# A selective-scan block: dt spread for two units at a time on the two 64-row halves of TensorE, with four dt banks and a dense ring of two

## What is computed

```python
x = x + block(layernorm(x))      # block(u): h = u + mamba(rmsnorm(u)); h + mlp(rmsnorm(h))
x = x + ffn(layernorm(x))        # silu(x W1) * (x W3), Walsh-Hadamard transform, times W2
# mamba: z, x, B, C, dt_raw = split(u @ in_proj); dt = softplus(dt_raw @ dt_proj + b)
# 8 groups of 32 channels p, 32 states n:
#   h[g,p,n] = exp(dt[g,p] * A[g,p,n]) * h[g,p,n] + dt[g,p] * x[g,p] * B[g,n]     (step by step in time)
#   y[g,p]   = sum_n h[g,p,n] * C[g,n]
# y = (y + x * D) * silu(z), then out_proj; mlp: down(silu(gate) * up), 704 wide
```

## Time and profile before

| | us |
|---|---|
| median of 3 executions | 1326.49 |
| the profiled execution, its own time | 1327.35 |
| its span in the trace | 1325.6 |
| PE busy | 1094.1 (83%) |
| DVE busy | 1101.3 (83%) |
| POOL busy | 977.7 (74%) |
| ACT busy | 626.5 (47%) |

### The profile page before, as it was taken

The page is one execution under the profiler, slowest core; times in us unless marked ns, Lnnn a source line. Parts: engine busy times, 40 slices in busy tenths (PEclk is TensorE's granted clock), DMA queues, the critical chain, the costliest instruction groups (busy, mean ns, idle before and its releaser), DMA issues.

```text
span 1325.6 us, 14750 instructions
## 1 busy us (share of the span) xinstructions
PE 1094.1 (83%) x3848; PEld 551.6 (42%) x3848; DVE 1101.3 (83%) x1265; ACT 626.5 (47%) x1070; POOL 977.7 (74%) x596
## 2 busy tenths in 40 slices
PE   2476658999798987999698987999698988998888
PEld 1121123445344453435344453445344454445445
DVE  3389998899889998999889998999989998997222
ACT  3645455445554455545554454545554355442310
POOL 0489997877879786877888786877888788875100
PEclk9776779999899997999899997999899998999889
DMA  5797866655665657575756647574756557550000
GB/s 194 175 236 157 186 153 133 141 131 124 161 143 128 143 134 162 119 158 118 170 133 138 140 119 167 122 167 103 177 129 145 118 132 167 127 127 32 1 0 17
DMA packets 99512, 176.56 MB, mean 133 GB/s; under 512 B 12960, under 2 KB 21600, under 8 KB 98784
## 3 DMA queue, kind: packets, MB, share of 16 engines
q1 hardware_dynamic: 98272, 171.36, 56.2%
q0 software_dynamic: 1152, 4.19, 0.9%
HBM read 150.34 MB, written 8.39 MB: 120 GB/s over the span
## 4 chain that ended last, share of the span: by engine, by line
PE 34%; POOL 27%; issue 21%; ACT 7%; DVE 6%; DMA 3%; SPq 1%; POOLq 0%; DVEq 0%; ACTq 0%
POOL h_s L980 16%; PE p_r L456 9%; PE p_r L467 6%; PE p_r L462 6%; POOL bt_s L960 5%; PE p_dt L411 4%; PE p_y L422 3%; PE p_r L442 2%; DVE h_s L760 2%; DMA bt_s<-dx_rows 2%; PE p_r L473 2%; PE p_r L437 1%; ACT p_dt L549 1%; POOL carry L977 1%; POOL sp_l L994 1%
## 5 line engine op out<-in xcount | busy, mean ns | idle before, releaser
L980 POOL TENSOR_TENSOR h_s<-h_s,c_s 128x1024 f32<-128x1024 f32 x256 | 608.3, 2377 | 127.5 <-DVE h_s L760 117.2
L549 ACT ACTIVATE p_dt<-p_dt,an_s 128x512 f32<-128x512 f32 x512 | 333.1, 657 | 334.0 <-PE p_dt L411 333.5
L411 PE MATMUL p_dt<-kdt,pick_s 128*128 128x512 f32 x512 | 357.6, 704 | 106.9 <-DVE h_s L760 105.0
L760 DVE TENSOR_TENSOR_SCAN h_s<-p_dt,carry,bt_s 128x512 f32<-128x512 f32 x256 | 322.2, 1272 | 25.3 <-ACT p_dt L549 20.3
L760 DVE TENSOR_TENSOR_SCAN h_s<-p_dt,bt_s 128x512 f32<-128x512 f32 x256 | 304.9, 1210 | 31.0 <-ACT p_dt L549 17.7
L467 PE MATMUL p_r<-nT,w_s 128*128 128x512 f32 x512 | 243.2, 602 | 0.4 <-ACT nT L686 0.4
L960 POOL TENSOR_TENSOR bt_s<-bt_s,b_s 128x1024 f32<-128x1024 f32 x96 | 226.7, 2361 | 10.9 <-DMA bt_s<-dx_rows 10.5
L411 PEld LDWEIGHTS p_dt<-kdt,pick_s 128*128 128x128 f32 x512 | 103.4, 204 | 264.8 <-DVE h_s L760 180.7
L745 DVE TENSOR_TENSOR bt_s<-bt_s,p_b 128x1024 f32<-128x1024 f32 x160 | 192.7, 1204 | 4.5 <-issue 2.8
L456 PE MATMUL p_r<-nT,gu_s 128*128 128x512 f32 x352 | 169.4, 602 | 0.3 <-DVE th_s L905 0.3
L422 PE MATMUL p_y<-h_s,ysel_s 128*32 128x512 f32 x1024 | 150.6, 663 | 18.8 <-POOL h_s L980 18.8
(11 more groups left out here) (93 smaller groups left out, 900.7 us busy)
## 6 DMA issues: line engine op xcount, KB each, us to landing
bt_s<-dx_rows SPq DMA_DIRECT2D x512, 256.0 KB, 5.3
kdt<-st_dt SPq DMA_DIRECT2D x64, 128.0 KB, 3.2
tok<-in_x SPq DMA_DIRECT2D x8, 512.0 KB, 7.1
xr_s<-xb_s SPq DMA_DIRECT2D x64, 64.0 KB, 2.4
dx_rows<-sp_w SPq DMA_DIRECT2D x16, 256.0 KB, 2.0
b_s<-xb_s SPq DMA_DIRECT2D x64, 64.0 KB, 2.5
xo<-in_x SPq DMA_DIRECT2D x8, 512.0 KB, 3.9
out<-xo POOLq DMA_DIRECT2D x8, 512.0 KB, 3.4
```

The source lines that it names most:

```text
L411: nc.tensor.matmul(p_dt[DT_BANK[u]][:, :], sel, kdt[:, h, p // 16, :], start=True, stop=True)\
L549: A(p_dt[DT_BANK[u]][:, :], p_dt[DT_BANK[u]][:, :], ACT.Exp, scale=an_s[:, c:c + 1]).then_inc(a_dA, 1)
L760: V.tensor_tensor_scan(h_s[:, u % 8, :], p_dt[DT_BANK[u]][:, :], bt_s[:, u % 16, :], carry[:, u:u + 1] if par else 0.0, ALU.mult, ALU.add) ...
L980: G.tensor_tensor(h_s[:, two, :], h_s[:, two, :], c_s[:, h, :].unsqueeze(1).broadcast_to([P, 2, T]), ALU.mult)\
```

## The change

- Spread by pairs: in each even slot u PE issues units u + 2 and u + 3 together. One uses rows 0 to 63 of TensorE, the other rows 64 to 127 (`pick_s` and `kdt` sliced by 64 partitions), into two different banks of four.
- `kdt` is laid out anew, so that each 64-partition half holds high and low part of 32 rows; `load_dt` issues eight DMAs of 32 partitions in place of four of 64. `pick_s` is half as large and is loaded by four DMAs of together half the bytes in place of one.
- A pair waits until the scans of the units four and three back are over, at every place of a tile.
- PSUM has 8 banks: four for dt, one each for B and y, and two in place of three for the dense ring. The stages keep their slots.

```diff
-DT_BANK = [u % 3 for u in range(U - 1)] + [1]
-DT_GAP = [4, 2] + [3] * (U - 3) + [2]
...
-RING = 3
+RING = 2
...
-        p_dt = [bank(f"p_dt{k}") for k in range(3)]
+        p_dt = [bank(f"p_dt{k}") for k in range(4)]
...
-            sp.dma_start(bt_s[:, 0:4, :].rearrange("p a b -> p (a b)"), pick).then_inc(l_w["c"], 16)
+            for k in range(4):
+                quarter, part = slice(32 * k, 32 * k + 32), k % 2 * 1024
+                sp.dma_start(bt_s[quarter, 0:2, :].rearrange("p a b -> p (a b)"), pick[quarter, part:part + 1024])\
+                  .then_inc(l_w["c"], 16)
...
                 for part in range(2):
                     for q in range(2):
-                        sp.dma_start(kdt[64 * part:64 * part + 64, h, q, :].bitcast(F32),
-                                     st_dt[64 * q:64 * q + 64, part, :].bitcast(F32)).then_inc(l_k[h], 16)
+                        for b in range(2):
+                            dst, src = 64 * b + 32 * part, 64 * q + 32 * b
+                            sp.dma_start(kdt[dst:dst + 32, h, q, :].bitcast(F32),
+                                         st_dt[src:src + 32, part, :].bitcast(F32)).then_inc(l_k[h], 16)
...
-            def spread(i, u):
-
-                h, p = u // UH, unit_channel(u)
-                n = i * U + u
-                sel = pick_s[:, p % 16, :]
+            def spread_pair(i, u):
+
+                h, q, row, n = u // UH, u % 4 // 2, unit_channel(u) % 8, i * U + u
                 if u % UH == 0:
-                    pe.wait_ge(l_k[h], (i + 1) * 64)
-                if u >= 3 or from_tile(i, 1):
-                    pe.wait_ge(v_sc, n - DT_GAP[u] + 1)
-                nc.tensor.matmul(p_dt[DT_BANK[u]][:, :], sel, kdt[:, h, p // 16, :], start=True, stop=True)\
-                    .then_inc(pe_dt, 1)
+                    pe.wait_ge(l_k[h], (i + 1) * 128)
+                if u >= 4 or from_tile(i, 1):
+                    pe.wait_ge(v_sc, n - 2)
+                for b in range(2):
+                    half = slice(64 * b, 64 * b + 64)
+                    nc.tensor.matmul(p_dt[u % 4 + b][:, :], pick_s[half, row, :], kdt[half, h, q, :],
+                                     start=True, stop=True).then_inc(pe_dt, 1)
...
-                    if (units if u + 2 < U else pre):
-                        spread(i + (u + 2) // U, (u + 2) % U)
+                    if u % 2 == 0 and (units if u + 2 < U else pre):
+                        spread_pair(i + (u + 2) // U, (u + 2) % U)
```

More of the change, by code:

```diff
@@ L133, in build @@
         ident_s = sb("ident_s", [P, P])
-        pick_s = sb("pick_s", [P, 16, P], F32R)
+        pick_s = sb("pick_s", [P, 8, P], F32R)
         ysel_s = sb("ysel_s", [P, 60])
@@ L483, in transform_w2 @@
                 for k in range(4):
-                    ps = ring[k] if k < RING else p_y
+                    ps = ring[k] if k < RING else p_dt[k]
                     nc.tensor.matmul(ps[:, :], had_s, hd_s[:, 4 + k, :], start=True, stop=True).then_inc(w_w2, 1)
@@ L510, in _ @@
             pe.wait_ge(w_in, 2)
-            pe.wait_ge(l_w["c"], 80)
+            pe.wait_ge(l_w["c"], 128)
             bodies(pe, body)
@@ L522, in _ @@
                 A(in_s[:, k, :, :], in_s[:, k, :, :], ACT.Copy, scale=par_s[:, k:k + 1]).then_inc(w_in, 1)
-            act.wait_ge(l_w["c"], 80)
+            act.wait_ge(l_w["c"], 128)
             A(an_s[:, :], an_s[:, :], ACT.Exp).then_inc(w_an, 1)
@@ L541, in keep_w2 @@
                     act.wait_ge(w_w2, k + 1)
-                    src = (ring[k] if k < RING else p_y)[:, :].rearrange("p (b d) -> p b d", d=D)
+                    src = (ring[k] if k < RING else p_dt[k])[:, :].rearrange("p (b d) -> p b d", d=D)
                     A(w2_s[:, 2 * k:2 * k + 2, :], src, ACT.Copy).then_inc(w_w2c, 1)
@@ L548, in decay @@
                 c = UH * (u // UH) + unit_channel(u)
-                A(p_dt[DT_BANK[u]][:, :], p_dt[DT_BANK[u]][:, :], ACT.Exp, scale=an_s[:, c:c + 1]).then_inc(a_dA, 1)
+                A(p_dt[u % 4][:, :], p_dt[u % 4][:, :], ACT.Exp, scale=an_s[:, c:c + 1]).then_inc(a_dA, 1)
             def normalise(dst, src, scale, bias, signal):
@@ L586, in softplus @@
                     if h:
-                        act.wait_ge(l_k[0], (t + 1) * 64)
+                        act.wait_ge(l_k[0], (t + 1) * 128)
                     elif from_tile(t, 1):
-                        act.wait_ge(l_k[1], t * 64)
+                        act.wait_ge(l_k[1], t * 128)
                     act.wait_ge(g_dt, m + 1)
@@ L720, in _ @@
             dve.wait_ge(w_zero, 2)
-            dve.wait_ge(l_w["c"], 80)
+            dve.wait_ge(l_w["c"], 128)
             V.tensor_copy(pick_s[:, :, :].rearrange("p a b -> p (a b)"),
-                          bt_s[:, 0:4, :].rearrange("p a b -> p (a b)")).then_inc(w_pick, 1)
+                          bt_s[:, 0:2, :].rearrange("p a b -> p (a b)")).then_inc(w_pick, 1)
             def butterflies():
@@ L759, in scan @@
                     dve.wait_ge(pe_y, i * (U // 4) + u // 4 - 1)
-                V.tensor_tensor_scan(h_s[:, u % 8, :], p_dt[DT_BANK[u]][:, :], bt_s[:, u % 16, :],
+                V.tensor_tensor_scan(h_s[:, u % 8, :], p_dt[u % 4][:, :], bt_s[:, u % 16, :],
                                      carry[:, u:u + 1] if par else 0.0, ALU.mult, ALU.add).then_inc(v_sc, 1)
@@ L845, in body @@
                                 if h:
-                                    dve.wait_ge(l_k[0], (nt + 1) * 64)
+                                    dve.wait_ge(l_k[0], (nt + 1) * 128)
                                 elif from_tile(nt, 1):
-                                    dve.wait_ge(l_k[1], nt * 64)
+                                    dve.wait_ge(l_k[1], nt * 128)
                                 dve.wait_ge(a_dth, m + 1)
```

## The result

| | before | changed |
|---|---|---|
| median of 4 runs each, us | 1326.45 (1325.91 to 1327.89) | 1379.56 (1371.93 to 1384.34) |
| profiled execution, us | 1327.35 | 1371.93 |
| its span, us | 1325.6 | 1370.2 |
| mean granted PE clock | 0.919 | 0.895 |

The changed kernel is slower: ratio 1.0393, 95% interval 1.0345 to 1.0441, or +53 us. The forecast was 1346 us with a range up to 1366. The two profiles of it are +44.6 and +54.8 us over that of before; both are used.

What follows compares the result with a forecast made beforehand. It took PE and DVE to run neck and neck in the dense stages. Seven bodies (19.3 us), tail 1.3 and start 1.4, less 2 gained, made +20.0 on the median of 1326.49: 1346 us, range 1329 to 1366.

Steps and rivals of the forecast that it cites:

- w2: First w2 matmul waits for the read of w3 7, costing 0.25 us a tile.
- The ring of two: Stages wait for the reader two back; at gate 4 PE stands 2.4 us, charged at 1.7 us a tile.
- Tail: In the last body gate 4 and w2 0 each stand for one DVE read: 1.3 us.
- w1/w3: the new wait costs nothing: In w1/w3 the smallest slack before a needed read is 0.30 us, so the shorter ring costs nothing.
- z and the transposes: I charge nothing: z 0 and hT 1 wait for readers, but PE idles there for the norm chain: no charge.
- The pair of spreads: In w1/w3, a half-array pair between full matmuls takes 0.67 us, 0.21 more than before: 0.8 us a tile.
- the start: At the run's start, extra load_dt DMA issues cost 2.4 us, the pick load saves 1: +1.4 us.
- What is gained: At the tile's end the last w2 matmuls no longer stand behind PE's wait for scan 61: -2 us.
- Rival 1: The halves don't overlap: in w1/w3 and gate stages each pair costs 0.23 us more, 1364 us; chance 0.13.
- 3 (faster): Early spreads remove half of the scans' 38.0 us waiting and gate 4's bank is free in time: 1312 us; chance 0.12.
- Rival 2: The ring wait at gate 4 is hidden because DVE is late there: 7 x 1.7 us less, 1334 us; chance 0.17.

Runs made afterwards that it cites:

- e1: Kernel before with only the dense ring cut from three banks to two, one bank left unused: 1368.48 us, ratio 1.0316.
- e12: Kernel before with a ring of two, the idle bank serving as third ring bank for gate, up and dtp0 only: 1343.94 us, ratio 1.0138.
- e8: Kernel before with dtp0 moved ahead of gate 0 in the plan: 1345.01 us, ratio 1.0136.
- e6: Kernel before, without pairs, each spread alone on a 64-row half with the new layouts and loads: 1421.15 us, ratio 1.0711.
- e10: Kernel before with two xo buffers by tile parity, so loading x needn't wait for the last tile's store: 1327.21 us, ratio 1.0013.
- e2: Changed kernel with every spread on all 128 rows and the old layouts and loads: 1365.37 us, ratio 1.0305; repeated, 1363.40 us.
- e11: Changed kernel with two xo buffers by tile parity, so loading x needn't wait for the last tile's store: 1376.91 us, ratio 1.0378.
- e9: Changed kernel with each pair's matmuls issued three times in the bodies of tiles -1, 0 and 1: 1385.09 us, ratio 1.0428.
- e4: Kernel before with DVE's drive reading B from SBUF instead of the PSUM copy, ACT's copies dropped: 1488.02 us, ratio 1.1186.

## Why the prediction was wrong

The direction and most mechanisms were right; the sum came out at +20 where +53 was measured, and +49.7 in the mean of the changed kernel's two profiles. The 29.7 us between lie by the table in gate 3 (7.4 against nothing), in the tile's change with slots 63 and 0 to 12 together (+6.9 against -2), before w2 (5.7 against 1.75), in w1/w3 (8.3 against 5.6), in the tail (4.0 against 1.3), in gate 4 (14.0 against 11.9) and in smaller parts. No term of the sum has the clock. Point by point, with the table's numbers for e1 (the ring alone) and for the changed kernel:

- **"The ring of two", gate 4: right in size.** Forecast 1.7 us a tile from a 2.4 us hold; the change shows 1.35 and 1.77 in slots 22 to 25 of tiles 1 to 6, after a wait of 1.78. 7 x 1.7 = 11.9 stands against 10.6 (e1) and 13.2. The way was not quite the one forecast: scan 25 waits for ACT 0.64 us longer and not 1.7, the rest lies in the waits before scan 23 (0.68) and before DVE's read of gate 4 (0.74), and dtp0 has no wait for a read.
- **"The ring of two", gate 3: left out. This is the step that failed first.** I compared w1 4, gate 4, w2 and z with their readers, and not gate 3. The trace of before had it, in the same stretch as the earlier trace rows:

```profile
530.55 1.88 PE L456 MATMUL p_r<-nT,gu_s 128*128 128x512 f32 x4
531.97 0.66 DVE L905 SCALAR_TENSOR_TENSOR th_s<-th_s,p_r 128x512 f32<-128x512 f32 x1
```

  The last two of the four passes are gate 3; they began at 530.55 + 0.86 = 531.4, and the read of gate 2, whose bank they take with a ring of two, ended at 532.63, 1.2 us later. I had seen only that "gate 3 is read until 537.35". It costs 0.8 to 0.9 us a tile in e1 and about 1.0 in the change, since a state sum stands behind it and the scan waits for that: 6.0 and 7.4 us in slots 19 to 22 against nothing in the sum.
- **"Tail" and the seventh body: too small.** The sum had 7 like bodies and 1.3 us of tail. Tile 7 has 3.5 us in slots 22 to 25 and 2.0 before w2, where tiles 1 to 6 have about 1.5 and 0.45. The gate 4 wait of tile 7 is 2.75 us, and the clock takes 1.1 of the 3.5 (e1, where it did not fall there, has 2.4). The tail is 3.7 (4.3 in e1, 1.7 in e12). Runs with a ring of three have +0.8 (e8), -1.4 (e6) and -2.8 (e10) in the tail, so its parts are no firmer than some 2 us.
- **"w1/w3: the new wait costs nothing": nearly.** No wait of PE for a read is recorded there, and e1 and e12 have 0.4 us in slots 40 to 44 of each of the tiles 2 to 6, 2.0 in all. There DVE waits 0.66 us for ACT's tanh before its read of a w1 stage (593.21 in e1's timeline) where it waited 0.27 before: DVE arrives earlier against PE, and no bank is waited for.
- **"w2": 0.25 us forecast, 0.3 to 0.5 measured**, 5.7 in all against 1.75.
- **"z and the transposes: I charge nothing", the cover being the norm chain: right for the ring alone but for tile 1, wrong for the change.** Slots 0 to 12 cost 4.7 in e1, of which 3.3 are tile 1, and 3.5 in e12, all of it in tile 1; 2.3 of that lie in slots 3 to 6, where the first profile of the changed kernel has 0.1. With pairs they cost 8.7 and 12.7 (e2), in the change 10 and 15. In the row at 667.20 PE stands 2.59 us for the out block's add before z 0, as named, with DVE's and ACT's own chain behind. The load of x sets a small part of it at most: e11 gains 3.2 us there in three tiles.
- **"The pair of spreads": sizes right, sum too small.** 0.63 against 0.67 for a pair, 9.12 against 9.20 for four slots, the overlap real (two 64-row spreads are 0.50 us of busy PE together, and e1's timeline has 0.50 for one full spread where nothing runs beside it). In slots 36 to 48 of tiles without a fall of the clock the ring costs 0.39 us, the pairs on full rows 0.25 more (e2) and the halves 0.40 more (changed): 0.65 for pairs on halves against 0.8 forecast. But the halves cost 15 us by medians, against a forecast of 5.6 for the pairs and 1.4 for the start. The table shows 8.9 of them between the means of the two profiles each (49.7 and 40.9): 3.3 in slots 36 to 48, 2.4 in 12 to 19 (1.3 of it in tile 0, at the clock of 0.5; e9, where the clock came back, has none of that; for the rest I charged nothing "since PE will stand there anyway"), 1.2 before w2, 1.1 at the start, the rest scattered. The other 6 are not found in the profiles; one of the e2 profiles was the slowest of its runs (1371.93 against a median of 1363.40), one of the changed kernel's the fastest (1371.93 against 1379.56). The lower mean clock with the halves (0.890 to 0.898 against 0.915 to 0.923) is a likely cause, and that part stays open.
- **"What is gained": -2 forecast.** PE's wait before the last spread fell from 5.74 to 4.18 and slot 63 got 5.7 us shorter, more than forecast, all of it from the pairs (e1 has -0.1, e2 -5.7). With it comes a longer start of the next tile: slots 0 to 12 are +4.7 in e1 and +8.7 and +12.7 in e2. The largest gain, 3.45 us at the end of tile 3, stands before the largest loss, 3.8 to 7.1 us in slots 0 to 12 of tile 4. That one causes the other was argued, not shown; the pairs' net gain of 3 to 5 us is within the noise.
- **The rivals.** Rival 1 (no overlap) and 3 (faster) fell. Rival 2 (the wait at gate 4 hidden) fell with them: slots 22 to 25 have 10.6 us in e1 and 0.0 in e12.
- **The range** ended at 1366 because I let it close on rival 1. Several ring waits adding up was not among the cases, nor was the clock.

## What to carry to other kernels

When a buffer ring is made shorter, hold every stage's start against the end of its new predecessor's read, all of them in a table, in a middle body and in the last one too; the one left out here was worth about half of the one that was found. An order of work tuned for one number of buffers is not the best for another, and banks should be weighed in both directions before they are moved. A pair of half-array matmuls between full-size ones cost 0.63 us here, and the two full ones that it replaced 0.46: the switches have to be set against what the overlap saves, at the place where the pair stands. And a change that lets the matmul engine stand more can lower its clock; look at the granted clock of each stretch before the rest of a difference is put down to waits.

## What the runs showed of the hardware that was not expected

- DVE's 128x1024 fp32 multiply took 1204 ns with one operand in PSUM and 2273 ns with both in SBUF, while POOL's own multiply of the same shape rose from 2361 to 2672 ns. The Trainium skill (SBUF — State Buffer, Who interferes with whom) says that a DVE instruction with two SBUF inputs contends with a GpSimd instruction that reads SBUF; the trace agrees, and shows that both pay. Single multiplies of DVE took 1192 to 3791 ns in e4, and 1182 to 1222 before. So `p_b`, a bank spent on a copy of something that is in SBUF anyway, earns 161 us in this kernel.
- A spread on 64 rows between full matmuls costs 0.39 us more than one on 128 rows (e6), and a pair of them together only 0.63 against 0.46 for two full ones. The Trainium skill (TensorEngine Tiling, Key Properties) says that changing the tiling mode drains TensorE; by rows 0.19 to 0.22 us each way here.
- The granted clock of PE in 130 to 195 us was 0.71 before, 0.56 in the changed kernel with 1.0 us less PE work, and 0.72 with 5.2 us more (e9), between the levels of 1.2 and 2.4 GHz. It rose with PE's work, although e9 was no faster as a whole. In tile 7 of the changed kernel eight passes of w1/w3 took 5.40 us at a clock of 0.68 and 3.70 at 1.00.
